# Value products issued two steps behind their scores instead of one, in a four-layer attention kernel on one core

## The chip, the core and the metric

The program runs on one core of a Trainium2 chip. Its engines work side by side, each through its own queue in order: TensorE (PE, with its weight loads PEld), VectorE (DVE), ScalarE (ACT), GpSimd (POOL), and SyncE (SP), which issues the DMAs. They wait for one another only by semaphores. The metric is the device time of one execution in microseconds (us), from first to last instruction and the little that lies around it. Lower is better.

## The reference, cut to what matters

Eight images of 256 channels by 1024 pixels pass through four layers, each adding its result to what came in:

```python
x = L0(x)  # group norm, attention between channels: softmax over 32x32 logits per head
x = L1(x)  # one head: s = query.T @ key; attn = softmax(s); y = value @ attn.T; o = Wo @ y * gamma + x
x = L2(x)  # group norm, 8 heads of 32 channels: sim = q.T @ k (1024 x 1024); out = softmax(sim * scale) @ v.T; x + proj(out)
x = L3(x)  # the same kind as L2, added to the normalised input instead of x
```

Nearly all work is in layers 2 and 3: for each of 8 heads a 1024 x 1024 matrix of scores, its exponentials, their sums, and the product with the values. The softmax subtracts a row's maximum, which is found by a second pass of the same score product.

## The kernel before, in words

**Groups, steps, slots.** A group (layer, g) is four heads and 512 queries: four groups in layer 2, four in layer 3; layer 1 has one head and two groups. A group of layers 2 and 3 has 8 steps of 128 keys, a group of layer 1 has 2 steps of four blocks of 128 keys. A step is four slots, numbered j = 0 to 3, so a group has 32 slots, or 8 in layer 1. A slot is one score product on PE (L1261, into one of `SCORE_BANKS` = 2 banks), one exponential on ACT (L896, into `prob[...][:, j, :]`), and beside it usually one product for the maxima of a later group (L1232, read by DVE at L1016; three banks).

**Values and sums.** When a step is complete, its four value products (L1284; L1280 in layer 1) are issued together. The exponentials of the 8 steps of a group are also added up on POOL (L794, into `acc`): seven adds per group, each over 128 x 2048 elements, the first of them reading the tiles of steps 0 and 1. The exponentials of a step live in one of `PROB_SLOTS` = 4 buffers, reused four steps later: the exponentials of step s + 4 wait for the value products and the add of step s (step s = 0 for add 1).

**The end of a group.** A group's last value products are followed by `evacuate` (ACT copies the values bank), and by three pieces with fixed distances in slots: `finish` after 4 (PE multiplies `acc` by ones, L1305, which waits for the group's last add, and add 1 of the next group waits for it since there is one `acc`), `invert` after 6 (DVE transposes that result, L1040, takes the reciprocal and transposes back, L1044), `scale` after 9 (POOL multiplies the values by it, L772).

**The plan.** `plans()` writes one list of events per turn, and every engine walks that same list, taking what is its own. `group_sequence()` says which pieces lie beside which slots: projections (`side ... qk`, `v`, `out`), group norms (`stats`, `norm`, `mean`, `power`, `apply`), the channel attention of layer 0 (`rows`, `turn`, `gram`, ...). Pieces that need a scaled group (`out`) are put behind its `scale`, by `SCALED` = 16 or by slots written out. There are five turns: two for the first image, one between, the steady one as a loop over six images, and one for the end.

**Side banks.** All side pieces, `finish` and `maxrow` share two PSUM banks in strict turns (`SIDE_BANKS` = 2): a piece waits until the reader of the piece two before it has freed the bank. For `finish` that reader is the first transpose of `invert`.

**Lag.** Score events push the value events of their step on the list `late`. At the end of a step the loop takes from it while it is longer than `LAG` = `HPT` = 4, so the values of step s - 1 stand behind the scores of step s. Since `finish`, `invert` and `scale` count from the last values, `finish` of a group stands at the end of slot 7 of the next group, `invert` at slot 9, `scale` at slot 12.

Of the kernel before, what the change touches and what calls it, by code (L numbers as in the profile page):

```python
# [16 lines left out]
T = C // P  # L17
HEADS = 8
DH = C // HEADS
HPT = P // DH  # L20
QW = 512
NQ = N // QW
# [15 lines left out]
STEPS = {1: KC // HPT, 2: KC, 3: KC, LAST3: KC}  # L38
MAXIMA = {1: QT * NQ, 2: HPT * QT * NQ, 3: HPT * QT * NQ, LAST3: HPT * QT * NQ}

LAG = HPT
FINISH_AFTER = 4
INVERT_AFTER = 6
SCALE_AFTER = 9
SCALED = 16
LAST_PIECE = 30


# [49 lines left out]
def after_layer1(rest=True):  # L98
    more = split_operand(2, 0) + split_operand(2, 1) + side(2, "v", KC // 2)
    return side(1, "out", T * NQ) + [("save",)] + normalise(2) + (more if rest else [])  # L100
# [20 lines left out]
def spread(first, last, pieces):  # L121

    pieces = cut(pieces)
    return [(first + (last - first) * (2 * i + 1) // (2 * len(pieces)), x) for i, x in enumerate(pieces)]


def group_sequence():
    end = LAST_PIECE
    out2, out3 = side(2, "out", T * NQ), side(3, "out", T * NQ) + [("store", 3)]
    out1 = after_layer1(False)  # L130
# [5 lines left out]
    def at(slots, pieces):  # L136
        return [*zip(slots, pieces)]
# [4 lines left out]
    def rows(layer, g, slot):  # L142
        return (layer, g, None, None, slot, slot)
# [21 lines left out]
    def layer2_begins(pieces):  # L165
# [12 lines left out]
               [(2, 2, 8, 32, 0, 17), rows(2, 2, 19), (1, 0, 0, 8, 24, 27), rows(1, 0, 31), (1, 1, 0, 8, 28, 31)]),  # L178
              (1, 0, [], [rows(1, 1, 3), (2, 3, 0, 8, 0, 7)]),
              (1, 1, [], [(2, 3, 8, 16, 0, 7)]),  # L180
              (2, 2, at((12, 13, 14, 15, 16), out1[:T * NQ + 1])
               + at((17, 17, 18, 18, 19, 21, 24, 28, 29, 30, 31), out1[T * NQ + 1:]),
               [(2, 3, 16, 32, 0, 15), rows(2, 3, 19)]),
              (2, 3, spread(0, 14, early2) + spread(14, end, early_halves),
               [(2, 0, 0, 32, 14, 29), rows(2, 0, 31)])]
# [2 lines left out]
    steady = (layer2(True, True)  # L188
              + [(3, 0, spread(0, 14, late3) + spread(SCALED, end, out2),
                  [(3, 1, 8, 16, 0, 7), (1, 0, 0, 8, 8, 15), rows(1, 0, 19), (1, 1, 0, 8, 16, 23), rows(1, 1, 27),  # L190
                   (3, 1, 16, 24, 24, 31)]),
                 (1, 0, [], [(3, 1, 24, 32, 0, 7)]),
                 (1, 1, [], [rows(3, 1, 3), (3, 2, 0, 8, 0, 7)]),
                 (3, 1, at((12, 13, 14, 15, 16), out1[:T * NQ + 1])
                  + at((17, 17, 18, 18, 19, 21, 24, 28, 29, 30, 31), out1[T * NQ + 1:]),
                  [(3, 2, 8, 32, 0, 23), rows(3, 2, 27), (3, 3, 0, 8, 24, 31)]),
                 (3, 2, spread(0, 20, early2), [(3, 3, 8, 32, 0, 23), rows(3, 3, 27), (2, 0, 0, 8, 24, 31)]),
                 (3, 3, spread(0, end, side(2, "v", KC // 2)),
                  [(2, 0, 8, 32, 0, 23), rows(2, 0, 27), (2, 1, 0, 8, 24, 31)]),
                 (2, 0, spread(0, 14, late2) + spread(SCALED, end, out3),  # L200
                  [(2, 1, 8, 32, 0, 23), rows(2, 1, 27), (2, 2, 0, 8, 24, 31)])])
    out4 = side(LAST3, "out", T * NQ) + [("store", LAST3)]
    early4, late4 = (split_operand(LAST3, m) + split_operand(LAST3, m + 1) for m in (0, 2))
    last = (layer2(True, False)
            + [(3, 0, spread(0, 14, late3) + spread(SCALED, end, out2),
                [(3, 1, 8, 32, 0, 23), rows(3, 1, 27), (3, 2, 0, 8, 24, 31)]),
# [4 lines left out]
                [(LAST3, 0, 8, 32, 0, 23), rows(LAST3, 0, 27), (LAST3, 1, 0, 8, 24, 31)]),  # L211
               (LAST3, 0, spread(0, 14, late4) + spread(SCALED, end, out3),
                [(LAST3, 1, 8, 32, 0, 23), rows(LAST3, 1, 27), (LAST3, 2, 0, 8, 24, 31)]),
# [15 lines left out]
def plans():  # L229
    out, late, pending = [], [], []  # L230
    clock = 0

    def close(plan, pieces):

        while [x[0] for x in plan if x[0] in ("begin", "side")][-1:] == ["begin"]:
            plan += flat([pieces.pop(0)[1]])

    def advance(plan):

        x = late.pop(0)  # L240
        plan.append(x)
        if x[0] == "values" and x[3] == STEPS[x[1]] - 1:
            plan.append(("evacuate",) + x[1:3])
            pending.extend((clock + after, (kind,) + x[1:3]) for kind, after in
                           (("finish", FINISH_AFTER), ("invert", INVERT_AFTER), ("scale", SCALE_AFTER)))

    turns = group_sequence()
    for groups in turns:
        plan = []
        for at, (layer, g, pieces, maxima) in enumerate(groups):  # L250
            if layer is None:
                while late:
                    advance(plan)
                plan += [x for _, x in pending] + flat(pieces if ("max", 2, 0, 0) in pieces else cut(pieces))
                pending.clear()
                if at + 1 < len(groups) and groups[at + 1][0] == 1:
                    to = groups[at + 1][:2]
                    plan += [("max",) + to + (a,) for a in range(MAXIMA[to[0]])] + [("split",) + to, ("maxrow",) + to]
                continue
            slots = STEPS[layer] * HPT  # L260
            pieces = sorted(pieces, key=lambda x: x[0])
            for slot in range(slots):
                s, j = slot // HPT, slot % HPT
                plan.append(("score", layer, g, s, j))
                late.append(("values", layer, g, s) if j == HPT - 1 else ("value", layer, g, s, j))
                turning = []
                for to_layer, to_g, start, stop, low, high in maxima:
                    if start is None:
                        if slot == low:
                            turning.append(("maxrow", to_layer, to_g))  # L270
                    elif low <= slot <= high:
                        of, n = high - low + 1, stop - start
                        plan += [("max", to_layer, to_g, start + a)
                                 for a in range(n * (slot - low) // of, n * (slot - low + 1) // of)]
                        if slot == high and stop == MAXIMA[to_layer]:
                            plan.append(("split", to_layer, to_g))
                while pending and pending[0][0] <= clock:
                    x = pending.pop(0)[1]
                    (turning if x[0] == "finish" else plan).append(x)
                while pieces and (pieces[0][0] <= slot or slot == slots - 1):  # L280
                    plan += flat([pieces.pop(0)[1]])
                if turning:
                    close(plan, pieces)
                    plan += turning
                while j == HPT - 1 and len(late) > LAG:
                    advance(plan)
                clock += 1
        for x in [x for x in plan if x[0] == "finish"]:
            at, inverted = plan.index(x), plan.index(("invert",) + x[1:]) if ("invert",) + x[1:] in plan else -1
            after = [i for i in range(at + 1, inverted) if plan[i][0] in ("side", "maxrow", "finish")]  # L290
            if len(after) > 1:

                plan.insert(after[0] + 1, plan.pop(inverted))
        events = [x for x in plan if x[0] in ("begin", "side")]
        assert all(("side",) + x[2:] in (y, ("side",) + y[2:]) for x, y in zip(events, events[1:]) if x[0] == "begin")
        out.append(plan)
    assert not late and not pending
    return out
# [1058 lines left out]
```

## Time and profile before

| | |
|---|---|
| median of 3 runs | 3209.09 us (3201.22 to 3209.5) |
| the profiled execution | 3209.68 us, of which span 3207.9 us |
| PE busy | 2847.0 us, 89% |
| POOL busy | 2337.4 us, 73% |
| DVE busy | 1855.6 us, 58% |
| ACT busy | 1555.9 us, 49% |
| mean granted TensorE clock | 0.94 |

The busy shares are means over unlike stages. A steady image takes 375 us; the first image lies before about 520 us of the span and the last one behind 2770 us. In the waits, "A <- B" is idle time of A that ended when B was done; an idle engine costs time only where PE comes to wait for it. The granted clock is 1.0 at 2.4 GHz and 0.5 at 1.2 GHz.

### The profile page before, as it was taken

The numbers are of one execution on the slowest core, as the hardware profiler recorded it, in microseconds if no ns is written. First come the engines' busy times: TensorE is split into PE (matmuls) and PEld (weight loads), VectorE is DVE, ScalarE is ACT, GpSimd is POOL, SyncE is SP. The second block draws the span as 40 slices with busy tenths as digits, with TensorE's granted clock in tenths as the row PEclk, the third lists the DMA queues.
The fourth block names the chain that finished last, engine by engine and source line by source line (L and its number), as shares of the span: only waits on it lengthen the run. The fifth ranks groups of instructions, "written<-read, shape, count | busy, mean of one in ns | idle before, by whom it ended". The sixth has DMA issues, their size and how long they took to land.

```text
span 3207.9 us, 47035 instructions
## 1 busy us (share of the span) xinstructions
PE 2847.0 (89%) x12872; PEld 1415.6 (44%) x12872; DVE 1855.6 (58%) x3293; ACT 1555.9 (49%) x2794; POOL 2337.4 (73%) x781
## 2 busy tenths in 40 slices
PE   5669879999989989999989999899889999998986
PEld 3335434554445444454435544354444544443432
DVE  0245537557664666556665666656665566756661
ACT  1214445455554455545554555544555455555553
POOL 3215657678876787868876788767878688888887
PEclk9779979999999999999999999999999999999997
DMA  1051034233340334330343324403343303524320
GB/s 59 24 76 20 24 54 72 37 51 53 44 82 13 41 55 69 55 47 19 45 80 40 51 48 49 81 13 41 55 69 55 51 16 45 82 37 49 40 36 14
DMA packets 74160, 151.73 MB, mean 47 GB/s; under 512 B 9073, under 2 KB 10609, under 8 KB 73906
## 3 DMA queue, kind: packets, MB, share of 16 engines
q1 hardware_dynamic: 73906, 148.56, 30.4%
q8 instruction: 133, 2.18, 0.3%
q14 instruction: 121, 0.99, 0.1%
HBM read 20.46 MB, written 16.78 MB: 12 GB/s over the span
## 4 chain that ended last, share of the span: by engine, by line
PE 61%; issue 10%; POOL 9%; DMA 8%; ACT 5%; DVE 5%; SPq 1%; ACTq 0%; POOLq 0%; DVEq 0%
PE psum L1261 14%; PE psum L1284 11%; PE psum L1232 10%; POOL acc L794 8%; PE psum L1207 5%; DMA Q<-lo 5%; PE psum L1176 4%; PE psum L1184 4%; PE psum L1280 3%; ACT prob L896 2%; DMA K<-hi 2%; DVE maxpart L1016 2%; PE psum L1118 2%; PE psum L1305 2%; SPq L707 1%
## 5 line engine op out<-in xcount | busy, mean ns | idle before, releaser
L794 POOL TENSOR_TENSOR acc<-acc,prob 128x2048 f32<-128x2048 f32 (+1 forms) x480 | 1871.2, 3898 | 236.6 <-ACT prob L896 207.0
L1016 DVE TENSOR_REDUCE maxpart<-psum 128x1 f32<-128x512 f32 x2176 | 1409.7, 684 | 902.6 <-PE psum L1232 874.0
L896 ACT ACTIVATE prob<-psum 128x512 f32<-128x512 f32 x2176 | 1227.7, 597 | 1058.9 <-PE psum L1261 1026.8
L1261 PE MATMUL psum<-Q,K 104*128 104x512 f32 x2048 | 1093.3, 536 | 105.6 <-ACT prob L896 61.3
L1232 PE MATMUL psum<-K,Q 96*128 96x512 f32 x2048 | 839.4, 413 | 73.2 <-DMA K<-hi 59.5
L1261 PEld LDWEIGHTS psum<-Q,K 104*128 104x128 f32 x2048 | 398.1, 195 | 816.0 <-ACT prob L896 409.4
L794 POOL TENSOR_TENSOR acc<-prob 128x2048 f32<-128x2048 f32 (+1 forms) x80 | 312.2, 3903 | 460.5 <-PE psum L1305 310.0
L1284 PE MATMUL psum<-prob,vT 128*32 128x512 f32 x4096 | 587.4, 634 | 0.0
L1232 PEld LDWEIGHTS psum<-K,Q 96*128 96x128 f32 x2048 | 404.4, 198 | 209.5 <-issue 100.2
L1284 PEld LDWEIGHTS psum<-prob,vT 128*32 128x32 f32 x4096 | 102.6, 111 | 208.6 <-ACT prob L896 121.4
L1176 PE MATMUL psum<-ha,wqkv_sb 128*128 128x512 f32 x288 | 153.4, 624 | 9.4 <-ACT ha L818 9.4
L1305 PE MATMUL psum<-acc,ones 128*32 128x512 f32 x640 | 91.2, 643 | 50.9 <-POOL acc L794 50.9
L1207 PE MATMUL psum<-att,wp_sb 128*128 128x512 f32 x256 | 131.8, 606 | 3.4 <-POOL att L772 3.4
L772 POOL TENSOR_TENSOR att<-att,turned_sums 128x512 f32<-128x512 f32 x80 | 102.3, 1279 | 43.0 <-DVE turned_sums L1044 43.0
L1280 PE MATMUL psum<-prob,products 128*128 128x512 f32 x256 | 118.7, 607 | 0.0
L1176 PE MATMUL psum<-hb,wqkv_sb 128*128 128x512 f32 x224 | 118.2, 614 | 0.0
L983 DVE SCALAR_TENSOR_TENSOR lo<-psum,cols_sb,hi 128x512 fp32r<-128x512 f32 x64 | 48.0, 751 | 115.8 <-ACT hi L846 115.8
L1040 DVE STREAM_TRANSPOSE turned_sums<-psum 128x512 f32<-128x512 f32 x80 | 56.6, 708 | 79.8 <-PE psum L1305 79.6
L753 POOL TENSOR_TENSOR rstd<-gvar,half_power 128x2 f32<-128x2 f32 x24 | 16.8, 701 | 105.5 <-DVE gvar L963 105.5
L877 ACT COPY att<-psum 128x512 f32<-128x512 f32 x80 | 47.0, 588 | 93.3 <-PE psum L1280 52.7
L983 DVE SCALAR_TENSOR_TENSOR lo<-psum,hi 128x512 fp32r<-128x512 f32 x64 | 44.2, 690 | 67.8 <-ACT hi L846 67.7
L846 ACT ACTIVATE hi<-psum,cols_sb 128x512 fp32r<-128x512 f32 x64 | 44.1, 689 | 76.4 <-DMA Q<-lo 44.2
(115 smaller groups left out, 1956.2 us busy)
## 6 DMA issues: line engine op xcount, KB each, us to landing
Q<-hi SPq DMA_DIRECT2D x128, 256.0 KB
K<-hi SPq DMA_DIRECT2D x128, 256.0 KB
Q<-lo SPq DMA_DIRECT2D x64, 256.0 KB
K<-lo SPq DMA_DIRECT2D x64, 256.0 KB
xa<-in_x SPq DMA_DIRECT2D x8, 1024.0 KB, 8.4
scratch<-xa SPq DMA_DIRECT2D x8, 1024.0 KB, 4.1
xb<-scratch SPq DMA_DIRECT2D x8, 1024.0 KB, 5.0
out<-hb SPq DMA_DIRECT2D x7, 1024.0 KB, 5.4
```

Source lines behind the costliest of these rows:

```text
L772: pool.tensor_tensor(dst, dst, turned_sums[:, :, :].rearrange("p a c -> p (a c)"), ALU.mult).then_inc(group_done, 1)
L794: pool.tensor_tensor(total, first if a == 1 else total, this, ALU.add).then_inc(added, 1)
L896: act.activation(prob[STEP_STARTS.slot(b, start)][:, j, :], score_bank[(SCORES.rank[b.n][e] - 1) % SCORE_BANKS], ACT.Exp, scale=1.0 if lay ...
L1016: dve.tensor_reduce(maxpart[layer][:, a // NQ, a % NQ:a % NQ + 1], bank, AX_X, ALU.max).then_inc(max_free, 1)
L1176: ins = pe.matmul(side_bank, wqkv_sb[layer][:, t, o:o + P], normed[layer][:, t, part], start=(t == 0), stop=(t == T - 1))
L1184: ins = pe.matmul(side_bank[:, a * width:(a + 1) * width], src[:, t, kt * P:(kt + 1) * P], w[:, t, o:o + width], start=(t == 0), stop=(t = ...
L1207: ins = pe.matmul(side_bank, w[:, t, ot * P:(ot + 1) * P], src[:, t, part], start=(t == 0), stop=(t == T - 1))
L1232: pe.matmul(max_bank[(r - 1) % MAX_BANKS], left, right, start=True, stop=True).then_inc(max_full, 1)
L1261: pe.matmul(score_bank[(r - 1) % SCORE_BANKS], left, right, start=True, stop=True).then_inc(score_full, 1)
L1280: ins = pe.matmul(values_bank, vT1[:, kt, :], slot[:, j, :], start=(kt == 0), stop=(kt == KC - 1))
L1284: ins = pe.matmul(values_bank[head_rows(j), :], vT[layer][:, s, head * DH:(head + 1) * DH], slot[:, j, :], start=(s == 0), stop=(s == KC - 1),
L1305: ins = pe.matmul(side_bank[head_rows(j), :], ones[:, :], acc[:, 0 if layer == 1 else j, :], start=(layer == 1 or POOLED == KC), stop=True ...
```

## The change

The lag is doubled: the values of step s - 2 stand behind the scores of step s. With the values, `evacuate`, `finish`, `invert` and `scale` move 4 slots later, to slots 7, 11, 13 and 16 of the next group, and on POOL the adds of a step stand 4 slots later in the plan. `SCALED` goes from 16 to 19, so the `out` pieces of layers 2 and 3 lie in slots 19 to 30 instead of 16 to 30. In the group behind layer 1 the pieces that follow its end move by 1 to 4 slots: four `out` from slots 12-15 to 16-19, `save` 16 to 20, four `stats` from 17, 17, 18, 18 to 20, 20, 21, 21, `norm` 19 to 22, `mean` 21 to 24, `power` 24 to 27, four `apply` from 28, 29, 30, 31 to 29, 30, 31, 31. Where the plan drains `late` between groups (behind layer 1 of the first image, and at the very end) the pieces pending from an earlier group are written out before a new group's first values.

```diff
-LAG = HPT
+LAG = 2 * HPT
 FINISH_AFTER = 4
 INVERT_AFTER = 6
 SCALE_AFTER = 9
-SCALED = 16
+SCALED = 19
...
-              (2, 2, at((12, 13, 14, 15, 16), out1[:T * NQ + 1])
-               + at((17, 17, 18, 18, 19, 21, 24, 28, 29, 30, 31), out1[T * NQ + 1:]),
+              (2, 2, at((16, 17, 18, 19, 20), out1[:T * NQ + 1])
+               + at((20, 20, 21, 21, 22, 24, 27, 29, 30, 31, 31), out1[T * NQ + 1:]),
...
-                 (3, 1, at((12, 13, 14, 15, 16), out1[:T * NQ + 1])
-                  + at((17, 17, 18, 18, 19, 21, 24, 28, 29, 30, 31), out1[T * NQ + 1:]),
+                 (3, 1, at((16, 17, 18, 19, 20), out1[:T * NQ + 1])
+                  + at((20, 20, 21, 21, 22, 24, 27, 29, 30, 31, 31), out1[T * NQ + 1:]),
...
                 while late:
+                    if late[0][0] == "value" and late[0][3:] == (0, 0):
+                        plan += [x for _, x in pending]
+                        pending.clear()
                     advance(plan)
```

## Rows read from the trace of the kernel before

**Rows 1.** Waits of all engines over the whole span: total us, times, longest.

```profile
POOL acc L794 <- PE psum L1305: 310.0, 70, 14.5
...
PE psum L1305 <- POOL acc L794: 50.9, 13, 7.6
```

**Rows 2.** Waits of PE from 500 to 2768 us, the steady images, same columns.

```profile
PE psum L1261 <- ACT prob L896: 46.2, 84, 1.6
...
PE psum L1093 <- ACT mv L860: 12.3, 6, 2.1
PE psum L1305 <- POOL acc L794: 11.4, 6, 2.8
```

**Rows 3.** Waits of PE from 2768 us to the end, the last image.

```profile
PE psum L1305 <- POOL acc L794: 36.5, 6, 7.6
```

**Rows 4.** PE by time (start, us): a finish, a bare step, the next score.

```profile
3079.40 1.06 PE L1305 MATMUL psum<-acc,ones 128*32 128x512 f32 x8
...
3081.25 0.50 PE L1261 MATMUL psum<-Q,K 104*128 104x512 f32 x1
...
3084.68 0.50 PE L1261 MATMUL psum<-Q,K 104*128 104x512 f32 x1
```

**Rows 5.** POOL by time in the last image: three first adds, then six more.

```profile
2774.52 4.56 POOL L794 TENSOR_TENSOR acc<-prob 128x2048 f32<-128x2048 f32 x1
...
2928.32 4.57 POOL L794 TENSOR_TENSOR acc<-prob 128x2048 f32<-128x2048 f32 x1
...
3080.64 4.58 POOL L794 TENSOR_TENSOR acc<-prob 128x2048 f32<-128x2048 f32 x1 [2.85 <-PE psum L1305]
...
3086.42 28.07 POOL L794 TENSOR_TENSOR acc<-acc,prob 128x2048 f32<-128x2048 f32 x6
```

**Rows 6.** PE by time: the first product of two passes of the loop.

```profile
1271.45 0.76 PE L1261 MATMUL psum<-Q,K 104*128 104x512 f32 x1 [5.53 <-issue]
...
1646.08 0.77 PE L1261 MATMUL psum<-Q,K 104*128 104x512 f32 x1 [6.27 <-issue]
```

**Rows 7.** PE and DVE by time: second slot behind a finish, then its invert.

```profile
1323.23 0.40 PE L1232 MATMUL psum<-K,Q 96*128 96x512 f32 x1
...
1324.40 0.71 DVE L1040 STREAM_TRANSPOSE turned_sums<-psum 128x512 f32<-128x512 f32 x1
```

**Rows 8.** PE and ACT by time: norm of layer 2, steady image.

```profile
1510.56 0.39 PE L1093 MATMUL psum<-mv,const_sb 128*128 128x4 f32 x2 [2.05 <-ACT mv L860]
...
1519.25 0.81 ACT L818 ACTIVATE ha<-xa,gb,ga 128x512 f32<-128x512 f32 x1
...
1522.81 0.81 ACT L818 ACTIVATE ha<-xa,gb,ga 128x512 f32<-128x512 f32 x1
...
1523.67 1.13 PE L1176 MATMUL psum<-ha,wqkv_sb 128*128 128x512 f32 x2 [0.67 <-ACT ha L818]
```

**Rows 9.** ACT by time: a projection's copy that waits for a DMA.

```profile
1436.80 0.69 ACT L846 ACTIVATE hi<-psum,const_sb 128x512 fp32r<-128x512 f32 x1 [1.56 <-DMA Q<-lo]
```

**Rows 10.** POOL, DVE and PE by time: layer 1's end in the first image.

```profile
126.47 1.27 POOL L794 TENSOR_TENSOR acc<-prob 128x512 f32<-128x512 f32 x1 [9.24 <-PE psum L1305]
...
127.40 0.71 DVE L1044 STREAM_TRANSPOSE turned_sums<-inverse 128x512 f32<-128x512 f32 x1
...
136.13 1.27 POOL L772 TENSOR_TENSOR att<-att,turned_sums 128x512 f32<-128x512 f32 x1
136.32 1.94 PE L1305 MATMUL psum<-acc,ones 128*32 128x512 f32 x8 [2.96 <-POOL acc L794]
```

**Rows 11.** PE by time in the last image: three of its finishes.

```profile
2768.92 1.07 PE L1305 MATMUL psum<-acc,ones 128*32 128x512 f32 x8
...
2922.71 1.07 PE L1305 MATMUL psum<-acc,ones 128*32 128x512 f32 x8
...
3114.63 1.93 PE L1305 MATMUL psum<-acc,ones 128*32 128x512 f32 x8 [6.64 <-POOL acc L794]
```

## The prediction, made before the changed kernel was run

> **What bounds the kernel now.** I read the waits of all engines first, then PE's own waits stage by stage, then PE, POOL and DVE by time around a few `finish` products. PE is busy 89% of the span, so what counts is PE's idle time and who ends it. The pair that the change speaks to is in [rows 1]: POOL's first add of a group waits 310.0 us in all for `finish`, and PE's `finish` waits 50.9 us for POOL's last add. The 310 us cost nothing by themselves, since POOL has time to spare in a steady image. The 50.9 us are PE's, and they are the most that a later `finish` can save by waiting less.
>
> Where they lie matters. From 500 to 2768 us, the steady images with the end of the first, PE waits there six times, 11.4 us in all and 2.8 at most [rows 2]. The last image has six more, 36.5 us, up to 7.6 each [rows 3]; a small wait of 3 us is in the first image's drain. In the last image there is little side work: a step whose scores start at 3081.25 is followed by the next at 3084.68, so a bare step takes PE 3.43 us [rows 4]. One add takes POOL 4.56, or 28.07 / 6 = 4.68 us in a row of six [rows 5]. So POOL is the slower engine there, while a steady image repeats every 1646.08 - 1271.45 = 374.6 us [rows 6], 5.5 us for each of its 68 steps, and is PE's. What PE still waits for in it is small: 46.2 us for exponentials in 84 places of all six images [rows 2].
>
> **Part 1, the values themselves: 0.** The same value products run in the same batches. They never waited for an exponential: the scores ahead of them already wait, two banks back, for later ones. That two-bank wait is the cover, and it stays. So issuing values later frees nothing on PE. What the change really moves is everything counted from the last values.
>
> **Part 2, `finish` four slots later, steady images: -11.4 us.** POOL's last add has one more step of at least 3.43 us [rows 4], more than the largest of the six waits, 2.8 us [rows 2]. That POOL then starts add 1 a step later is covered by its spare time: seven adds and a `scale` take 33.9 us (3086.42 + 28.07 - 3080.64) [rows 5] and a group of PE 8 x 5.5 = 44.
>
> **Part 3, the side banks behind `finish`: +9.9 us.** All side pieces share two banks in turns, so the second one behind `finish` needs `invert`'s first transpose. At slots 7 to 9 the pieces are sparse. At slot 11 of group (2, 2) they are not: `rows 0` stands in slot 12, `rows 1` in slot 13, the same slot as `invert`, and `rows 1` needs `finish`'s bank. DVE transposes only after the maximum of slot 13. In [rows 7] that slot's product starts at 1323.23 and PE could go on 0.23 us later, while the transpose ends at 1324.40 + 0.71 = 1325.11: PE would stand 1.65 us. Only the steady turn has this, 6 x 1.65 = 9.9. The bounds are 0, if what follows was to wait anyway, and 2.2 each (13 in all), if DVE comes a maximum later. I take 1.65, the row's own distances.
>
> **Part 4, the norm of layer 2: +4.9 us.** `mean` already makes PE wait 2.05 us for ACT, and PE waits 0.67 us for the last `apply` [rows 8]. From the first `out` to `mean` there were 9 slots and are 8: PE arrives one bare slot, 3.43 / 4 = 0.86 us, sooner, and DVE has one maximum of 0.69 less to do; net +0.2. The four `apply` had four slots and have three. Before, they take 1522.81 + 0.81 - 1519.25 = 4.37 us [rows 8]; now the first starts a slot later (+0.86) and one exponential less stands between them (-0.4), so PE's wait grows by 0.5. Together 0.7 us, 7 times (six steady images and the first), 4.9. Queued behind ACT's `apply` are its next exponentials, and PE's scores behind those. Bounds: 0 and 1.4 each, the double.
>
> **Part 5, the other neighbours: 0.** In (3, 0) and (2, 0) `invert` now stands behind a projection's low half on DVE, which waits for ACT's copy at 1436.80, itself waiting for a DMA [rows 9]; PE passes this point at that DMA's time in both kernels. The `out` pieces at slot 19 stand some 7.7 us behind the start of `finish` (3084.68 - 3079.40 = 5.3 and three quarters of a step's scores), and the `scale` is done after 1.2 + 4.56 + 1.27 = 7.0 us [rows 4, 5, 10]. Without these covers it is up to 1 us in each of 14 groups. SP's DMAs keep their order; `save` is four slots later, with its load a whole group away. On POOL `power` of layer 2 now stands behind add 3 instead of add 4, so POOL waits for it some 4 us, out of its spare time; the adds behind it are not late for slot 11.
>
> **Part 6, the drain behind layer 1 of the first image: +2.9 us.** Nothing hides POOL there. Before, the seven short adds of (1, 1) run from 126.47 to 136.13, right behind `finish` of (1, 0), and its `scale` comes after them [rows 10]. Now that `scale` stands ahead of them. It can start when `invert` is done, at 127.40 + 0.71 = 128.1, ends 1.27 later at 129.4, and the adds end at 129.4 + 9.66 = 139.1 instead of 136.1. `finish` of (1, 1) waits for them, and the whole chain of the drain for that. I take 2.9; bounds 1.3 (the `scale` alone) and 4.
>
> **Part 7, the last image: -4.5 us.** Its end hangs on POOL: 33.9 us of work per group and a handover of 3080.64 - 3079.40 = 1.2 us make 35 us from `finish` to `finish`, whatever PE does [rows 4, 5]. A later `finish` doesn't remove the six waits. They turn into waits for buffers, as ACT's step s + 4 needs add s. What changes is how POOL's chain starts. It starts one step and one `finish` later, 3.4 + 0.9 = +4.3 us. But at two places `power`, which needs a mean of slot 8, stood ahead of add 1 and behind `finish`: from 2768.92 to 2774.52 and from 2922.71 to 2928.32 it is 5.6 us from `finish` to add 1 [rows 5, 11], 4.4 more than the 1.2. With `finish` at slot 11 `power` is done by then: -8.8. Together -4.5. Bounds: +4.3, if `power` was covered anyway, and -9, if five handovers become faster as well (see the clock).
>
> **The sum.** -11.4 + 9.9 + 4.9 + 2.9 - 4.5 = +1.8 us on the profiled execution of 3209.68, so 3211.5. That execution lies 0.6 above the median of the runs shown; I forecast 3211.
>
> **Clock.** The `finish` behind a wait of 6.64 us takes 1.93 us, the ones without a wait 1.07 [rows 11], so a long wait costs about 0.9 us more at the handover, which is on POOL's chain. If the waits are cut into pieces of 4.68 - 3.43 = 1.25 us per step, that may go. The Trainium skill, page "TensorE: Matmul & The Clock Gate", section "Part 1: The HAM clock gate", says that the lower clock is the default state and that activity releases the throttle. By that rule (the trace agrees, 1.93 against 1.07) the change would save 5 x 0.9 = 4.5 us more in the last image. It is part of rival (a), not of the forecast, since the small pieces might be enough to keep the clock low as well.
>
> **The rivals.** (a) The gain without the new waits: `rows 1` and the `apply` are absorbed, and five handovers run at full clock: 3209.7 - 11.4 + 2.9 - 4.5 - 4.5 = 3192. For it: PE has other small waits in which new ones could vanish [rows 2]. Against: PE is the saturated engine, and nothing ahead of `rows 1` waits. All 50.9 us at once would give 3159; POOL's chain of 35 us speaks against that, and I give it 0.02.
>
> (b) The other side: the ring of four buffers becomes the wait. With `finish` at slot 11, add 1 must be done before the fifth step's first exponential. From the start of `finish` add 1 needs 1.24 + 4.56 = 5.8 us. The score whose exponential needs that buffer starts 5.28 us after it and takes 0.5, 5.8 too [rows 4, 5]. Before, there was a whole step between. It decides from there: any delay of POOL beyond it stops ACT, and with its two banks PE. At 0.6 us in 50 of the 80 groups that is +30, thus 3241. For it: the margin is zero in a bare step. Against: most steady steps carry side work and take 5.5 us, and PE has two scores ahead. The Trainium skill, page "Perfetto Trace Analysis", section "Identifying Performance Opportunities", says that the same gap repeated on the engine that should be saturated can mean too few buffers. By that rule such a gap would stand at slot 16 of the lean groups; no row of before shows one there.
>
> (c) The side banks cost more than I found: 1.65 us in three more groups of each image, 6 x 3 x 1.65 = +30, also 3241. By the plan, the other groups have at least three slots between `finish` and the piece that needs its bank.
>
> **How the numbers follow.** Forecast, 3200 to 3219: 0.55. Rival (a) 0.19, with 3159 beside it 0.02. Rivals (b) and (c) together 0.24, from 3220 to 3241 and beyond. The 8-in-10 range reaches from 3190 to 3234. A measurement of this kernel can tell about 0.3%, 9.6 us, from no change; so faster 0.20, same 0.56, slower 0.24.
>
> **What would show it.** PE's waits for POOL before L1305 should be gone in the steady images and far smaller in the last, while ACT's waits for POOL's adds grow in the last. In each steady image a PE wait of 1.65 us should stand before `rows 1` (L1106), ended by DVE's L1040. Add 1 should start 1.2 us after `finish` also behind `power`. The loop should repeat in 374.6 to 376 us; under 373.5 would refute parts 3 and 4, over 378 would speak for (b) or (c), told apart by whether ACT waits for POOL or PE for DVE.

## The result, and the profile after

The changed kernel takes 3239.13 us (median of four runs, 3234.07 to 3241.35) and the kernel before, on the same chip, 3205.16 (3201.22 to 3209.5). The ratio is 1.0101, with an interval of 1.0081 to 1.0121: slower by 1.0%. The forecast was 3211, which would have been too small a change to tell, and the upper end of its range was 3234. The profiled execution took 3241.35 us with a span of 3239.6, against 3209.68 and 3207.9.

The difference is first laid out by stage. A pass of the loop begins with its first score, as in [rows 6]; in the kernel after, two of those rows are:

```profile
1283.80 0.77 PE L1264 MATMUL psum<-Q,K 104*128 104x512 f32 x1 [5.97 <-issue]
...
1664.11 0.76 PE L1264 MATMUL psum<-Q,K 104*128 104x512 f32 x1 [7.42 <-issue]
```

That is 380.3 us for a pass, where it was 374.6. In the same way the starts of the first score of every group give this table (us of the profiled executions; a group's time runs to the start of the next group, mean of the six passes; 1 stands for layer 1's (1, 0) and (1, 1) with (3, 1), through which its late values move):

```
            to the loop  a pass  last image | (2,1) (2,2) (2,3) (3,0)    1  (3,2) (3,3) (2,0)
before            523.2   373.3       445.1 |  38.5  52.9  52.4  43.7  62.4  41.8  33.9  47.6
after             527.0   378.8       439.5 |  40.3  52.7  52.3  46.0  61.8  41.8  34.1  49.7
```

Another execution of the changed kernel (e11 below) gives group means that differ from these by up to 0.7 us, and a pass of 378.2; so differences of some tenths in one group say nothing.

The first image (+3.8) and the last (-5.6) came out near the forecast (+2.9 and what the first image has of part 4; -4.5). The loop did not: +5.5 us in each of six passes, +33 in all, in three groups: (2, 1), (3, 0) and (2, 0).

The waits of PE in the steady images, the view of [rows 2], first after, then a row of before that stood behind those shown:

```profile
PE psum L1264 <- ACT prob L899: 50.4, 64, 1.8
...
PE psum L1235 <- DVE maxpart L1019: 17.1, 39, 0.8
PE psum L1096 <- ACT mv L863: 11.5, 6, 1.9
PE psum L1109 <- DVE turned_sums L1043: 8.9, 6, 1.5
PE psum L1179 <- ACT ha L821: 8.3, 6, 1.4
```

```profile
PE psum L1232 <- DVE maxpart L1016: 8.8, 24, 0.6
```

The 11.4 us of `finish` waiting for POOL are gone, as forecast. A new row of 8.9 us stands for `rows 1`, as forecast. Not forecast: waits for DVE's maxima twice as long (17.1 for 8.8) and 4.2 us more for exponentials, in fewer places. ACT's wait for the transfers of the projections' halves (the copy `hi` waits until the stacked operand of an earlier piece has left) grew too. ACT's waits in the same stretch, after and before:

```profile
ACT hi L849 <- DMA Q<-lo: 76.4, 30, 4.1
```

```profile
ACT hi L846 <- DMA Q<-lo: 51.7, 16, 3.8
```

Last, PE's busy time over the six passes (start and end; length, then busy time of PE, PEld, DVE, ACT and POOL with counts; PEclk, DMA share, GB/s), after and before:

```profile
527.00:2800.00 2273.00, 2102.74 (x9624) 1049.06 (x9624) 1391.68 (x2466) 1165.33 (x2094) 1733.91 (x571) 0.96 0.33 49
```

```profile
523.00:2763.00 2240.00, 2082.38 (x9629) 1042.57 (x9626) 1393.67 (x2467) 1165.09 (x2094) 1736.18 (x571) 0.97 0.33 49
```

The loop is 33 us longer, and 20.4 us of that is PE *busy* longer with the same products: they ran at the lower clock more often. By the granted clock of the two traces the loop has 198 us at 1.2 GHz where it had 154; 44 us more at half speed are 22 us of work not done, about the 20.4. Only 12.6 us is idle time (170.3 against 157.6). My sum had counted idle time alone.

### The profile page after: what moved, and what is told of

It is laid out like the page before. It is cut to its first block, busy times and chain, and to the rows that moved or that the text cites. A ratio compares the mean times of both kernels' runs of the same rounds, so it can differ in the third digit from the quotient of the medians.

```text
span 3239.6 us, 47035 instructions
## 1 busy us (share of the span) xinstructions
PE 2862.8 (88%) x12872; PEld 1419.6 (44%) x12872; DVE 1853.1 (57%) x3293; ACT 1556.1 (48%) x2794; POOL 2338.3 (72%) x781
## 4 chain that ended last, share of the span: by engine, by line
PE 55%; issue 16%; POOL 9%; DMA 8%; DVE 5%; ACT 4%; SPq 1%; POOLq 0%; ACTq 0%; DVEq 0%
PE psum L1264 13%; PE psum L1235 10%; PE psum L1287 9%; POOL acc L797 7%; PE psum L1179 5%; PE psum L1210 4%; PE psum L1187 4%; DMA Q<-lo 4%; DVE maxpart L1019 2%; DMA K<-hi 2%; DMA Q<-max_rows 2%; PE psum L1121 2%; ACT prob L899 2%; PE psum L1308 2%; DVE stats L933 1%
```

## The experiments

All ratios are to the kernel before, run on the same chip. The theory after the result (A): `finish` and `invert`, four slots later, stand beside other work of DVE and ACT, and the exponentials or maxima behind them come late. In the texts below A and B are the two outcomes that each expectation sets against each other. The rivals: the late values themselves, the moved `out` and norm pieces, the ring of four buffers.

**Which part of the change.** First, the values two steps late, but `finish` and `invert` near them, at slots 8 and 10:

```diff
-FINISH_AFTER = 4
-INVERT_AFTER = 6
+FINISH_AFTER = 1
+INVERT_AFTER = 3
```

> The changed kernel, but finish stands 1 slot and invert 3 slots behind the last values instead of 4 and 6: the values still run two steps behind their scores, while finish comes back to slot 8 and invert to slot 10 of the next group (they were at 7 and 9 before the change, at 11 and 13 with it); scale and all other pieces stay where the change put them. Theory A (the lag of the values is free, what costs is where finish and invert now stand among their neighbours): one pass of the loop takes 374.5 to 376.5 us instead of 380, the total is 3205 to 3217. Theory B (values two steps late hold the four exponential buffers and the queues longer, wherever finish stands): a pass stays at 379 to 381 us, the total at 3234 to 3242.

3237.64 us (3228.45 to 3248.94), ratio 1.0098 (1.0062 to 1.0134), a pass of 377.0. The total is B's, the pass lies between the two: (3, 0) at 43.0 and (2, 0) at 47.5 are back at the times of before, but `finish` now has to wait for POOL's last add in twelve places, in (2, 2) and (3, 2) of every pass, and (3, 2) lost 3.1 us:

```profile
PE psum L1308 <- POOL acc L797: 18.5, 12, 2.1
...
PE psum L1235 <- DVE maxpart L1019: 2.5, 7, 0.4
```

Second, the reverse, values as before and the end of a group late:

```diff
-SCALED = 16
+SCALED = 19
...
-                           (("finish", FINISH_AFTER), ("invert", INVERT_AFTER), ("scale", SCALE_AFTER)))
+                           (("finish", FINISH_AFTER + more[0]), ("invert", INVERT_AFTER + more[1]),
+                            ("scale", SCALE_AFTER + more[2])))
```

where `more` is (4, 4, 3), and (0, 0, 0) where the group that follows is one of layer 1.

> The mirror of the run before: the kernel before the change (values one step behind), but in all groups that are followed by a group of layer 2 or 3, finish stands 4 slots later (slot 11), invert at 13 and scale at 15, with out of layers 2 and 3 from slot 19. Theory A: a pass of the loop takes 378 to 381 us, as with the change, since the neighbours are the same; the total is 3225 to 3240. Theory B: 374 to 376 us per pass and 3200 to 3212 in all.

3249.15 us (3242.88 to 3262.02), ratio 1.0123 (1.0097 to 1.0149), a pass of 382.0; (2, 1), (3, 0) and (2, 0) at 39.5, 46.5 and 50.3. So the late end of a group suffices for the loss in (3, 0) and (2, 0), and for half of it in (2, 1). The total says less: the profiled execution, 3262.02 us, is the longest of the four, and 3.0 of its 8.7 us more a pass lie in the stretch with layer 1 (65.5 for 62.4), where this version makes `finish` wait for POOL's add six times, 8.1 us. Third, only the slots of the pieces behind it:

```diff
-SCALED = 16
+SCALED = 19
...
-                 (3, 1, at((12, 13, 14, 15, 16), out1[:T * NQ + 1])
-                  + at((17, 17, 18, 18, 19, 21, 24, 28, 29, 30, 31), out1[T * NQ + 1:]),
+                 (3, 1, at((16, 17, 18, 19, 20), out1[:T * NQ + 1])
+                  + at((20, 20, 21, 21, 22, 24, 27, 29, 30, 31, 31), out1[T * NQ + 1:]),
```

> The kernel before the change with only the slots of the out pieces and of the norm behind layer 1 moved as the change moves them (out from slot 19; behind layer 1 out at 16 to 19, stats to apply at 20 to 31). Theory A: 374.5 to 376 us per pass, 3204 to 3213 in all: my part 4 put the norm at 0.7 us per image, and the two traces show less. Rival C (denser out pieces and the squeezed norm are what costs): 378 to 380 us per pass and over 3225.

3209.54 us, ratio 1.0002 (0.9988 to 1.0017), a pass of 374.0: nothing in all. Only (3, 0), at 44.4 for 43.7, is somewhat longer.

**`rows` behind the inversion.** The changed kernel with

```diff
-            b += spread(12, end, side(0, "rows", 2) + side(0, "turn", KC // 2) + gram_to_logits)
+            b += spread(15, end, side(0, "rows", 2) + side(0, "turn", KC // 2) + gram_to_logits)
```

> The changed kernel with the pieces of the channel attention in group (2, 2) starting at slot 15 instead of 12, so that both rows pieces stand behind invert. Theory A: PE's wait for DVE's first transpose before rows 1 (8.9 us in six places) goes, and with it up to as much again by the clock: 1.5 to 2.5 us per pass, 3224 to 3232 in all. Rival D (the wait only moves to the next piece, as in a chain that is serial anyway): under 0.5 us per pass, 3236 to 3242.

3207.62 us (3204.82 to 3216.36), ratio 1.0009 (0.9994 to 1.0024): 31 us less than the changed kernel, over three times the length of the wait that went, and below the ranges of both theories. What surrounds the wait explains part of it. PE by time in the changed kernel, in the second and the third pass:

```profile
961.54 1.02 PE L1109 MATMUL psum<-wqk_sb,hsum 128*1 128x256 f32 x4 [1.48 <-DVE turned_sums L1043]
962.50 0.80 PE L1111 MATMUL psum<-rows_sb,count_n 1*1 1x256 f32 x2
963.23 0.80 PE L1264 MATMUL psum<-Q,K 104*128 104x512 f32 x1
963.82 0.63 PE L1235 MATMUL psum<-K,Q 96*128 96x512 f32 x1
...
966.94 1.94 PE L1287 MATMUL psum<-prob,vT 128*32 128x512 f32 x8
```

```profile
1342.50 1.02 PE L1109 MATMUL psum<-wqk_sb,hsum 128*1 128x256 f32 x4 [1.48 <-DVE turned_sums L1043]
1343.46 0.59 PE L1111 MATMUL psum<-rows_sb,count_n 1*1 1x256 f32 x2
1343.97 0.50 PE L1264 MATMUL psum<-Q,K 104*128 104x512 f32 x1
1344.31 0.40 PE L1235 MATMUL psum<-K,Q 96*128 96x512 f32 x1
...
1345.99 1.07 PE L1287 MATMUL psum<-prob,vT 128*32 128x512 f32 x8
```

The same wait of 1.48 us to the hundredth; behind it the score takes 0.80 us in one pass and 0.50 in the other, the eight value products 1.94 and 1.07. The granted clock says the same, in the view of stretches:

```profile
963.00:970.00 7.00, 7.00 (x26) 4.00 (x26) 1.47 (x3) 3.00 (x6) 6.92 (x3) 0.53 0.64 77
...
1344.00:1351.00 7.00, 6.73 (x40) 4.61 (x40) 3.46 (x5) 5.18 (x10) 6.92 (x3) 1.00 0.64 77
```

Step 3 of (2, 2) takes 7.9 us in the four passes where the clock stays up at this place, and 10.7 and 9.5 in the two where it falls; it took 6.3 to 6.4 before. With `rows` from slot 15 it takes 3.7 or 3.8 in all six; 2.1 us of that come back in steps 4 to 6, where the pieces now lie. The rest of the 31 us lies outside (2, 2), whose mean fell by 3.3 us a pass where the pass fell by 5.2: PE's busy time in the loop fell from 2102.74 to

```profile
529.00:2771.00 2242.00, 2085.53 (x9628) 1040.96 (x9624) 1389.92 (x2467) 1163.12 (x2094) 1733.96 (x571) 0.97 0.33 49
```

**The norm pieces of (2, 1) ahead of the finish.**

```diff
-            a += [(0, ("load",))] + at((10, 12, 14, 16, 17, 20, 23), normalise(0))
+            a += [(0, ("load",))] + at((9, 10, 11, 12, 17, 20, 23), normalise(0))
```

> The changed kernel with the four norm pieces of group (2,1), which stood at slots 10, 12, 14 and 16, at 9, 10, 11 and 12, so that VectorE has them behind it before the finish. Theory A, VectorE's backlog around the finish makes the 1.8 us that (2,1) lost: (2,1) at 38.5 to 39.2, the pass 377 to 377.7, the kernel 3228 to 3234 us. Theory B, the finish alone does it: (2,1) stays at 40.3 within 0.4, the kernel 3235 to 3243.

3224.40 us (3218.91 to 3233.5), ratio 1.0066 (1.0039 to 1.0092); (2, 1) at 38.4. Theory A, a little past its ranges, and 15 us in all, where the group's own 1.9 us a pass make 11.5. DVE by time in the changed kernel shows the jam:

```profile
918.83 0.68 DVE L933 BATCH_NORM_STATS2 stats<-xa 128x6 f32<-128x512 f32 x1
919.43 0.67 DVE L1019 TENSOR_REDUCE maxpart<-psum 128x1 f32<-128x512 f32 x1
920.02 0.70 DVE L1043 STREAM_TRANSPOSE turned_sums<-psum 128x512 f32<-128x512 f32 x1
920.76 0.25 DVE L1046 RECIPROCAL inverse<-turned_sums 128x16 f32<-128x16 f32 x1
921.05 0.71 DVE L1047 STREAM_TRANSPOSE turned_sums<-inverse 128x512 f32<-128x512 f32 x1
921.68 0.65 DVE L1019 TENSOR_REDUCE maxpart<-psum 128x1 f32<-128x512 f32 x1
922.26 0.67 DVE L933 BATCH_NORM_STATS2 stats<-xa 128x6 f32<-128x512 f32 x1
922.85 1.27 DVE L1019 TENSOR_REDUCE maxpart<-psum 128x1 f32<-128x512 f32 x2
924.04 0.68 DVE L933 BATCH_NORM_STATS2 stats<-xa 128x6 f32<-128x512 f32 x1
```

No row has an idle time: the inversion's 1.66 us (0.70 + 0.25 + 0.71) lie in the middle of four `stats` of 0.68 and their maxima. In the kernel before the inversion came ahead of the first `stats`. PE in the same stretch:

```profile
922.39 0.50 PE L1235 MATMUL psum<-K,Q 96*128 96x512 f32 x1 [0.64 <-DVE maxpart L1019]
923.58 0.51 PE L1235 MATMUL psum<-K,Q 96*128 96x512 f32 x1 [0.45 <-DVE maxpart L1019]
927.44 0.50 PE L1264 MATMUL psum<-Q,K 104*128 104x512 f32 x1 [1.76 <-ACT prob L899]
928.63 0.80 PE L1264 MATMUL psum<-Q,K 104*128 104x512 f32 x1 [0.34 <-ACT prob L899]
```

The longest, 1.76 us, is booked to ACT's exponential, but ACT itself stood before it, waiting for the `mv` that DVE makes behind the last `stats`:

```profile
925.54 0.67 ACT L863 ACTIVATE mv<-mv 128x1 f32<-128x1 f32 x2 [2.29 <-DVE mv L940]
```

With the norm moved ACT waits 1.59 us there and PE 1.17. But most of these waits are not new. The kernel before has them at the same pieces, 0.63 and 0.45 us for maxima and

```profile
919.25 0.50 PE L1261 MATMUL psum<-Q,K 104*128 104x512 f32 x1 [1.31 <-ACT prob L896]
```

PE's idle time in (2, 1) rose by 0.6 us a pass only, from 3.4 to 4.0; its time at the lower clock rose from 6.5 to 10.0 us a pass, and that is most of the 1.7 us. With the norm moved the two are 3.7 and 6.1.

**The last side pieces behind the finish.** Before `finish` the plan completes any side piece that has begun. With `finish` at slot 11 this pulls the second half of the last q and k piece, planned for slot 12, ahead of it, and ACT's copy of it waits for a transfer:

```profile
1068.00 0.69 ACT L849 ACTIVATE hi<-psum,const_sb 128x512 fp32r<-128x512 f32 x1 [4.03 <-DMA Q<-lo]
```

The kernel before did the same to another piece: its `finish` at slot 7 pulled the third of the four, planned for slot 8, and that copy waited nearly as long, in (3, 0) and in (2, 0) of every pass:

```profile
1053.94 0.69 ACT L846 ACTIVATE hi<-psum,const_sb 128x512 fp32r<-128x512 f32 x1 [3.75 <-DMA Q<-lo]
```

With the pieces spread to slot 16, all of them up to two slots later, the last begins behind `finish`:

```diff
-              + [(3, 0, spread(0, 14, late3) + spread(SCALED, end, out2),
+              + [(3, 0, spread(0, 16, late3) + spread(SCALED, end, out2),
...
-                 (2, 0, spread(0, 14, late2) + spread(SCALED, end, out3),
+                 (2, 0, spread(0, 16, late2) + spread(SCALED, end, out3),
```

and the same for (3, 0) and (LAST3, 0) of the last turn.

> The changed kernel with the side pieces of (2,0), (3,0) and (LAST3,0) spread over slots 0 to 16 instead of 0 to 14, so that the last half of the next image's q and k, whose ScalarE copy waits for a transfer (4.03 us, ScalarE hi<-Q<-lo at 1068.00 of the changed kernel), comes behind the finish. Theory A, this copy stands ahead of the finish's work and costs the 2.4 and 2.1 us that (3,0) and (2,0) lost: these groups back to 43.7 to 44.3 and 47.6 to 48.3 us, a pass of 374.5 to 376, the kernel 3212 to 3224 us. Theory B, the loss is the late finish's own (VectorE and ScalarE late for the exponential three slots on): the groups stay at 46.0 and 49.7 within 0.5, the kernel 3234 to 3242.

3208.49 us (3196.39 to 3221.48), ratio 1.0007 (0.9985 to 1.0029), a pass of 374.6; (3, 0) at 43.9 and (2, 0) at 47.6, theory A, with a total below its range. Steps 1 and 2 of each of these groups took 13.6 us together in the kernel before and 13.8 in the changed one, and take 10.5 here. In that kernel ACT's wait is 1.82 us in this place and 48.3 in all passes, and PE's wait for exponentials 30.2 for 50.4:

```profile
1061.69 0.69 ACT L849 ACTIVATE hi<-psum,const_sb 128x512 fp32r<-128x512 f32 x1 [1.82 <-DMA Q<-lo]
```

```profile
ACT hi L849 <- DMA Q<-lo: 48.3, 31, 3.0
```

```profile
PE psum L1264 <- ACT prob L899: 30.2, 52, 1.8
```

**All three together, and the same three in the kernel before.** Is this repair of the change, or would any layout gain by it? First the one move of `rows` in the kernel before:

> The kernel before with one change: the side pieces of group (2,2) start at slot 15 instead of 12, as in the run that gave the changed kernel 31 us. Theory A, those 31 us are a gain of the place of the side pieces and any layout would have it: (2,2) from 52.9 to between 49.5 and 51, a pass of 370 to 371.5, the kernel 3185 to 3195 us. Theory B, the place at 12 costs only where the values and the finish come late: (2,2) within 0.7 of 52.9, the kernel 3201 to 3211.

3210.68 us, ratio 1.0014 (0.9999 to 1.0029), (2, 2) at 52.0, 0.9 less than before, where B had allowed 0.7: theory B by the total, `rows` at slot 12 cost 31 us only where `invert` is at 13. Then the three moves in the changed kernel, with the pieces of (2, 0) in the second and third turn spread to slot 16 as well:

> The changed kernel with the moves of three runs together: side pieces of (2,2) from slot 15, those of (3,0) and (2,0) up to 16, norm of (2,1) at 9 to 12. If each removes its own loss: (2,1) 38.8, (2,2) 49.4, (3,0) 44, (2,0) 48, a pass of 368 to 370, the kernel 3178 to 3190 us, below both kernels. If only the side pieces of (2,2) count (theory B of the two others): 3203 to 3211.

3169.16 us (3164.01 to 3174.34), ratio 0.9880 (0.9854 to 0.9906): 70 us below the changed kernel, where the three moves alone gave 31.5, 30.6 and 14.7, together 77; the ratios to the kernel before, each on its own chip, add up without a rest (0.0092, 0.0094 and 0.0035 against 0.0221). Then, on one chip, the kernel before with the three moves, that version again, and the changed kernel again:

> The kernel before with the three moves that brought the changed kernel to 3169 us: side pieces of (2,2) from slot 15, those of (2,0), (3,0) and (LAST3,0) up to slot 16, norm of (2,1) at 9 to 12; values and finish as before. Theory A, the moves take neighbours out of the way of the finish's new place, so the old place gains little or loses: (2,1) 38.5 to 39.5, (2,2) 52 to 53, (3,0) 43.2 to 44.5, (2,0) 47 to 48.5 us, the kernel 3196 to 3214, and the late values themselves are worth 27 to 45 us once the neighbours are moved. Theory B, the moves are gains in any layout: the kernel 3160 to 3180.

> The changed kernel with the three moves, once more, beside the two others: 3162 to 3177 us, a ratio of 0.986 to 0.991 to the kernel before.

> The changed kernel as it is, for a comparison on one chip: 3232 to 3243 us, a ratio of 1.008 to 1.012. Its step 3 of group (2,2) takes 7.9 us in most passes and about 10 where the granted clock falls behind the wait of 1.48 us for the transpose; if the clock's falls follow the wait, they are again there in some passes, with none at this step in the run with the side pieces behind the invert (3.7 us in all six).

```
                     median us                ratio (interval)         a pass  (2,1) (2,2) (2,3) (3,0)    1  (3,2) (3,3) (2,0)
before               3209.30                  1
before + 3 moves     3180.43 (3176.5-3185.9)  0.9917 (0.9898-0.9936)    369.5   38.9  52.0  52.0  41.4  62.1  42.0  33.9  47.2
changed              3238.15 (3233.1-3246.9)  1.0100 (1.0080-1.0121)    378.2   39.8  53.2  51.7  46.3  61.8  41.9  34.1  49.4
changed + 3 moves    3165.83 (3160.6-3171.7)  0.9868 (0.9846-0.9890)    368.7   38.3  49.8  52.0  43.3  62.1  41.6  34.2  47.5
```

For the kernel before theory B held, 0.4 us past the end of its range: it gains 29 us. The group that gains most is (3, 0), 43.7 to 41.4, since the third piece is no longer pulled ahead of `finish`: ACT's wait for transfers in the loop falls from 51.7 us to 28.7. In (2, 0) steps 1 and 2 gain 3.1 us as well, but 2.8 come back behind them; (2, 2) gains 0.9 and the others 0.4 or less. So of the 72 us that the changed kernel gains by the moves, 29 are to be had without the change, and with its neighbours out of the way the change is worth 3180.43 - 3165.83 = 14.6 us, 0.5%. The last expectation held for the total. Step 3 of (2, 2) took 7.9, 10.7, 10.8, 7.9, 9.5 and 9.5 us in the changed kernel, so the clock fell in four passes of six, where 7.9 us had been expected in most; with the moves it took 3.7 or 3.8 in all six.

**What is left in (3, 0).** It stays at 43.3 us against 41.4 in the kernel before with the same moves. One candidate was the split of layer 1's maxima, four short DVE operations right behind the inversion:

```diff
-                  [(3, 1, 8, 16, 0, 7), (1, 0, 0, 8, 8, 15), rows(1, 0, 19), (1, 1, 0, 8, 16, 23), rows(1, 1, 27),
+                  [(3, 1, 8, 16, 0, 7), (1, 0, 0, 8, 8, 17), rows(1, 0, 21), (1, 1, 0, 8, 18, 23), rows(1, 1, 27),
```

> The changed kernel with the three moves and a fourth: in group (3,0) the split of the maxima for (1,0), four short VectorE instructions that stood at slot 15 right behind the inversion of the sums at slot 14, stands at slot 17, and their PE transposes at 21 instead of 19. Theory A, inversion and split together make VectorE late there (PE waits 0.42 and 0.77 us for maxpart at 1073.21 and 1075.31 of the changed kernel, and the granted clock falls behind it): step 4 of (3,0) from 8.2 to between 5.5 and 6.8 us, (3,0) from 43.3 to 41 to 42, the kernel 3148 to 3160 us. Theory B, the split costs the same 0.8 us of VectorE wherever it stands: (3,0) within 0.5 of 43.3, the kernel 3160 to 3174.

3169.58 us (3162.61 to 3171.89), ratio 0.9879 (0.9856 to 0.9901), (3, 0) at 43.6: theory B. Step 4 fell from 8.2 to 7.0 us and step 5 rose from 5.0 to 7.0. The other candidate was the distance of `finish` itself, with the three moves:

> The changed kernel with the three moves, and the finish at slot 8 and the inversion at slot 10 (FINISH_AFTER 1, INVERT_AFTER 3) behind values two steps late. Theory A, in (3,0) and (2,0) the late finish costs also where the last side piece is behind it: (3,0) from 43.3 back to 41 to 42 and (2,0) from 47.5 to 46 to 47, as with the kernel before and the same moves (41.4 in (3,0)); against that (2,2) and (3,2) get the wait for POOL's last add again, +2 to +4 us together; the kernel 3160 to 3176 us. Theory B, what is left in (3,0) belongs to the values themselves or to the output pieces at slot 19: (3,0) within 0.5 of 43.3, the kernel 3175 to 3190.

3248.49 us (3245.61 to 3249.3), ratio 1.0126 (1.0106 to 1.0147). (3, 0) stayed at 43.3, so B for that group, but the total is far outside both. A `finish` one slot behind late values waits for POOL's last add in (2, 2) and (3, 2) of every pass:

```profile
953.78 1.94 PE L1308 MATMUL psum<-acc,ones 128*32 128x512 f32 x8 [3.63 <-POOL acc L797]
```

```profile
PE psum L1308 <- POOL acc L797: 29.0, 12, 3.6
```

(2, 2) alone went from 49.8 to 56.0 us, 6.2 a pass, for a wait of 3.6 and the product behind it at the lower clock (1.94 for 1.06). So with the values two steps late and the neighbours moved, `finish` three slots nearer costs 83 us. In the loop 43 us of that are PE's busy time (2119.3 for 2076.5) and 23 its idle time.

## Why the prediction was wrong, point by point

**The first image and the last came out near the forecast.** In the last image the mechanism of part 7 is there: behind `power` the first add starts 1.24 us after `finish` (2810.85 to 2812.09, 2846.32 to 2847.56), where it took 5.6 [rows 5, 11].

```profile
2810.85 1.06 PE L1308 MATMUL psum<-acc,ones 128*32 128x512 f32 x8
...
2812.09 4.60 POOL L797 TENSOR_TENSOR acc<-prob 128x2048 f32<-128x2048 f32 x1 [0.31 <-PE psum L1308]
...
3147.47 1.94 PE L1308 MATMUL psum<-acc,ones 128*32 128x512 f32 x8 [2.37 <-POOL acc L797]
```

Three of the `finish` products still run at the lower clock, the one shown last (behind a wait of 2.37 us) and the two after it, at 3184.13 and 3219.97, behind 2.79 and 14.33; before there were five, and one of 1.50 us. PE's waits for POOL fell from 36.5 us to 22.6, of which 14.33 is the very last, and PE's waits for ACT's exponentials rose from 9.9 to 21.2, as described. -5.6 where -4.5 was forecast. Part 6 has the right sign and too small a size: the `finish` of (1, 1) comes at 143.51 instead of 136.32, 7.2 us later where 2.9 was forecast, because the `finish` of (1, 0) is itself 4.2 later (129.40 for 125.23); my sum had left it in its place. From the one to the other it is 14.1 us for 11.1, the 3.0 that the sum had priced at 2.9. Half of the 7.2 came back within the first image, which is 3.8 us longer. That this is so near the forecast is partly luck: the first score of layer 1, ahead of anything that changed, starts anywhere from 100.8 to 107.5 us in these runs, and in the other execution of the changed kernel the first image takes 522.3 us, less than before.

```profile
129.40 1.06 PE L1308 MATMUL psum<-acc,ones 128*32 128x512 f32 x8
143.51 1.93 PE L1308 MATMUL psum<-acc,ones 128*32 128x512 f32 x8 [5.98 <-POOL acc L797]
```

**Part 2 had the waits right and their price too small.** Six waits, 11.4 us, are gone, and steps 1 and 2 of (2, 2), where they lay, take 10.5 us for 13.5, so 18 us less in six passes.

**Part 3 had the place and the wait right, and missed what follows the wait.** 1.48 us six times, 8.9 for the forecast 9.9. But in two of six passes of one run, and four of six of another, the clock fell behind it, and step 3 took 1.6 to 2.9 us more for it. The whole move of `rows` is worth 31 us where I had priced 10. Parts 2 and 3 both lie in (2, 2), and the group came out as their sum says (-0.2 us a pass, forecast -0.25) only because both prices were too small, steps 3 to 6 taking 14 us more in six passes: that is luck.

**Part 4 had the waits right and their price wrong.** PE waits 1.38 us for an `apply` instead of 0.67, and 1.92 for `mean` instead of 2.05. These new slots alone cost nothing that can be measured (ratio 1.0002), so the 4.9 us are not in the end time. Probably what the wait was put in front of was late anyway; no run shows that.

**Part 5 is the step that failed.** It priced the other neighbours at 0, with a bound of 1 us a group. (2, 1) lost 1.7 us a pass and (3, 0) and (2, 0) 2.4 and 2.1, 37 us in six passes, more than the 33 that the loop lost. I had looked at the side banks and at when a transfer lands; I had not asked whom the inversion delays on DVE, an engine that is 58% busy on average but full in the stretch of (2, 1) where four `stats` stand. For (2, 1) its one move shows it. For (3, 0) and (2, 0) the versions with the values late and the end near, and the reverse, show that the late end of the group does it, but the copy that waits behind a pulled piece is not what was added: steps 1 and 2, where it lies, took 13.6 us before and 13.8 after. What was added lies in steps 3 to 6, 2.1 to 2.4 us in (3, 0) and 1.5 in (2, 0). Moving the pieces gains 3.1 to 3.4 us in steps 1 and 2, in both kernels, and so covers a loss that it does not remove. The Trainium skill, page "PSUM — Partial Sum Buffer", section "Engine vs sequencer instructions", says that the queues of ScalarE, VectorE and GpSimdE are strictly first in, first out. The trace agrees: the four exponentials behind the copy that waits 4.03 us (2.27 us together, at 1068.59) start only when it is done.

**For (3, 0) the cause is only half found.** The late end of a group makes it longer (46.5 with the end late and the values as before, 43.0 with the values late and the end near). Spreading the pieces to slot 16 gives 2.1 to 3.0 us with the change and 2.3 without. With that done in both, the changed kernel is still 1.9 us behind, and neither moving the split nor bringing `finish` nearer changed that. PE's idle time in the group rose by 1.4 us a pass, and two waits for DVE's maxima behind the inversion, in slots 17 and 19 of every pass, are 1.2 of it:

```profile
1073.21 0.50 PE L1235 MATMUL psum<-qk 96*128 96x512 f32 x1 [0.42 <-DVE maxpart L1019]
...
1075.31 0.76 PE L1235 MATMUL psum<-qk 96*128 96x512 f32 x1 [0.77 <-DVE maxpart L1019]
1075.87 3.33 PE L1210 MATMUL psum<-att,wp_sb 128*128 128x512 f32 x4
```

They stand also with the end late and the values as before (in four of six passes), and in neither the kernel before nor the version with the values late and the end near. But with the three moves the wait of 0.77 us stays even when the end is near, and where moving the split takes it away, one of 1.0 us for an exponential comes in slot 17. Behind them stands a whole `out` piece (3.33 us) in one slot, 19, whose halves lay in slots 16 and 18 before; the version with only the slots moved has that too, and its (3, 0) is 0.7 us longer. So the slots of `out` are a part; how the rest divides stays open.

**The clock paragraph treated the clock as a matter of the last image.** 20 of the 33 us are busy time at the lower clock. It stands in no single place, and I can't split it among the causes. The Trainium skill, page "TensorE: Matmul & The Clock Gate", section "Part 1: The HAM clock gate", says that activity releases the throttle and that its default state is the lower clock. The rows fit that, and show that a wait of 1.48 us with the same work around it costs the clock in some passes and not in others.

**The rivals.** (a) is refuted by the time, though half of its handovers at full clock came. (b) is real and small: ACT's waits for POOL's adds rose from 5.1 us to

```profile
ACT prob L899 <- POOL acc L797: 44.0, 38, 2.4
```

with 25.5 of it in the last image. In the loop they are 0.5 us in (2, 1) and 1.2 in (3, 1) and in (3, 3); (3, 3) lost 0.2 us and the stretch of layer 1 with (3, 1) nothing, and in (3, 0) and (2, 0) there is none. The version with three moves has 40.1 of the 44.0 left and is 72 us faster, so this was not the main cause. (c) named the wrong resource: no further side bank waits, but like (c) the loss came from new neighbours in three more groups. A pass of 378.8 us was over the 378 that I had set as the sign of (b) or (c); PE waiting for DVE, and not ACT for POOL, was the side it pointed to.

## What to carry to other kernels

When a piece is moved later, list for each engine what it now stands in front of, in the busiest group and not on average, and what the planner pulls along with it; this change cost 1% as it was, and gained 0.5% against an old version with the same neighbours moved. On an engine near saturation a wait can cost more than its length, since the products behind it may run at the lower clock (1.6 to 2.9 us more behind 1.48 us here): price busy time as well as idle time. And give the old version the same repairs before crediting the change with them: 29 of 72 us were there without it. The same holds for a cause seen in the new trace: look whether the old one has it too. ACT's wait of 4.03 us here had a twin of 3.75 in the kernel before.

## What the runs showed of the hardware that I had not expected

In steps 1 to 3 of (2, 2) in the changed kernel the passes of one execution repeat to 0.1 us (4.9, 5.6, 7.9), but for those where the clock falls, which are 1.6 to 2.9 us longer. And moving three pieces out of the way, 70 to 72 us in all, gave PE busy time back as well as idle time, the wait of 8.9 us before `rows 1` over three times its length: in the loop PE's idle time fell by 34.8 us (170.3 to 135.5) and its busy time by 26.2 (2102.74 to 2076.52) for the same products.

```profile
519.00:2731.00 2212.00, 2076.52 (x9625) 1039.83 (x9624) 1391.00 (x2466) 1163.24 (x2094) 1735.59 (x570) 0.97 0.33 50
```
